# A decoder layer on one core: a front in another order, cross-attention set-up inside the self-attention, the last pair's closing work split

## What is computed

```python
x = x + self_attention(layernorm(x))         # x: 32 sequences x 56 rows x 256; 16 query heads of 128, one key/value head, rotary, causal
x = x + cross_attention(layernorm(x), ctx)   # ctx: 32 x 1500 x 256, with a mask; 16 heads of 16; layernorm of the scaled result
x = x + ffn(layernorm(x))                    # gate, value and output layers of 1024, inputs to 8 bit, weights to -1, 0, 1
```

## Time and profile before

| | |
|---|---|
| median of 3 runs | 1477.72 us (1477.56 to 1482.31) |
| profiled execution, own time | 1479.29 us |
| its span | 1477.5 us |
| granted clock, mean | 0.97 |
| busy: PE, DVE, ACT, POOL | 93%, 68%, 49%, 30% |

### The profile page before, as it was taken

The page is one execution under the profiler, slowest core; times in us unless marked ns, Lnnn a source line. Parts: engine busy times, 40 slices in busy tenths (PEclk is TensorE's granted clock), DMA queues, the critical chain, the costliest instruction groups (busy, mean ns, idle before and its releaser), DMA issues.

```text
span 1477.5 us, 55098 instructions
## 1 busy us (share of the span) xinstructions
PE 1376.1 (93%) x25094; PEld 1176.1 (80%) x25094; DVE 1009.2 (68%) x1786; ACT 717.3 (49%) x939; POOL 442.2 (30%) x394
## 2 busy tenths in 40 slices
PE   3899999999299999999999999999999999999983
PEld 3687777786278888888888888888888888888871
DVE  4666666765044686877778687876877777677765
ACT  1444454443155555464555555555555555555540
POOL 2332232231032323333333333332323233232400
PEclk8899999999689999999999999999999999999995
DMA  7000000000422211212121121211112121111100
GB/s 210 1 2 25 5 1 29 1 2 1 107 58 58 56 50 45 61 31 75 48 59 48 44 62 31 75 50 57 48 44 61 30 76 59 47 48 44 48 6 3
DMA packets 38809, 66.75 MB, mean 45 GB/s; under 512 B 3605, under 2 KB 36818, under 8 KB 38578
## 3 DMA queue, kind: packets, MB, share of 16 engines
q1 hardware_dynamic: 38578, 63.24, 14.7%
HBM read 61.40 MB, written 1.84 MB: 43 GB/s over the span
## 4 chain that ended last, share of the span: by engine, by line
PE 68%; DVE 3%; issue 1%; POOL 0%; POOLq 0%; DVEq 0%
PE proj_ps L1196 19%; PE proj_ps L1187 18%; PE score_ps L1214 13%; PE sum_ps L1234 12%; PE side_ps L1265 3%; PE side_ps L1251 2%; PE side_ps L1279 1%; PE side_ps L1272 1%; PE side_ps L1258 0%; DVE amax L1072 0%; DVE exps L1019 0%; DVE inv L1031 0%; POOL low L894 0%; DVE vals L1010 0%; DVE hidden L1104 0%
## 5 line engine op out<-in xcount | busy, mean ns | idle before, releaser
L954 ACT ACTIVATE exps<-score_ps 125x1792 f32<-125x1792 f32 x192 | 320.6, 1670 | 418.8 <-PE score_ps L1214 418.8
L894 POOL TENSOR_TENSOR low<-raw,high 128x500 fp32r<-128x500 f32 x192 | 293.6, 1537 | 645.1 <-PE proj_ps L1187 510.3
L1019 DVE TENSOR_SCALAR exps<-exps,top 125x896 f32<-125x896 f32 x384 | 288.1, 792 | 18.0 <-ACT exps L954 17.5
L1214 PE MATMUL score_ps<-spread,keys 32*125 32x112 f32 x6144 | 218.9, 279 | 0.9 <-ACT exps L954 0.9
L1234 PEld LDWEIGHTS sum_ps<-exps,vals 125*32 125x32 f32 x12288 | 163.5, 110 | 47.6 <-issue 33.9
L1214 PEld LDWEIGHTS score_ps<-spread,keys 32*125 32x125 f32 x6144 | 184.8, 183 | 16.3 <-ACT exps L954 1.0
L1010 DVE COPY vals<-proj_ps 125x512 f32<-125x512 f32 x192 | 128.3, 688 | 96.8 <-PE proj_ps L1196 96.3
L1234 PE MATMUL sum_ps<-exps,vals 125*32 125x56 f32 x12288 | 192.0, 215 | 0.1
L1196 PE MATMUL proj_ps<-w_h,high 128*125 128x256 f32 x768 | 165.0, 296 | 0.0
L1187 PE MATMUL proj_ps<-high,w_h 128*128 128x500 f32 x384 | 132.8, 427 | 25.4 <-POOL low L894 25.4
L946 ACT ACTIVATE keys<-proj_ps,b_k 128x500 f32<-128x500 f32 x192 | 130.0, 677 | 52.4 <-PE proj_ps L1187 48.0
(11 more groups left out here) (129 smaller groups left out, 1668.2 us busy)
## 6 DMA issues: line engine op xcount, KB each, us to landing
raw<-in_ctxT SPq DMA_DIRECT2D x96, 500.0 KB, 3.7
w_q<-in_attn_Wq SPq DMA_DIRECT2D x4, 512.0 KB, 6.7
w_o<-in_attn_Wo SPq DMA_DIRECT2D x1, 2048.0 KB, 19.9
out<-y_out SPq DMA_DIRECT2D x16, 112.0 KB, 2.0
rows<-in_x SPq DMA_DIRECT2D x1, 1568.0 KB, 14.8
w_raw<-in_ffn_gate_wT SPq DMA_DIRECT2D x1, 1024.0 KB, 8.6
w_raw<-in_ffn_val_wT SPq DMA_DIRECT2D x1, 1024.0 KB, 5.0
w_raw<-in_ffn_out_wT SPq DMA_DIRECT2D x1, 1024.0 KB, 5.8
```

Source lines behind the costliest of these rows:

```text
L894: nc.gpsimd.tensor_tensor(low[r][:, k, :], raw[ring][:, k, :], high[r][:, k, :].bitcast(F32), ALU.subtract).then_inc(low_ready, 1)
L954: nc.scalar.activation(exps[t % 2][:, :, :, :].rearrange("p h r n -> p r h n"), score_ps[0:TILE, :, 0:2 * QW].rearrange("p r (h n) -> p r ...
L1019: nc.vector.tensor_scalar(tile, tile, LIMIT_LO, top[:, n, at:at + 1], ALU.max, ALU.min)\
L1214: ins = nc.tensor.matmul(score_ps[0:TILE, r, to:to + HE * S], keys[c % 2][32 * r:32 * r + 32, k, (at + half) * TILE:(at + half + 1) * TILE ...
```

## The change

In block A, the first load of `x` covers four pairs in place of two, and `w_kv` is loaded ahead of `cos`, `sin` and `causal`. The statistics of group 1 come right behind the keys' rotary, those of group 2 behind query unit 3, and those of group g + 3 in the odd pair of group g (`norm_stats`, with `power1` on POOL). The unit `norm` of group 1 lies between query units 3 and 4. In pair 0, PE works off query units 2 and 3 of group 1 ahead of the first turn. `sines` writes over `swapped` in place of `by_sin`, and `outT` is one buffer in place of two.

Buffers of block B that are filled early now belong to a class `Early`, outside both blocks. The raw buffer of the feed-forward weights is one of them, and holds the first two chunks once the weights are quantised. `w_f` and the small inputs are loaded behind the first raw weights; two memsets move to POOL's start in block A. In pair 15, ACT splits the weights and chunk 0 behind the exponentials (`split_high`), POOL does the low part of chunk 0 and the spreads behind `power(14)`, and DVE does `w_l`, the mask's limits and the scaled bias (`set_up`) behind `norm2_rows(14)`. Block B starts with the load of chunk 2, the high and low part of chunk 1 and PE's first projection.

In block B, `divide(15, 0)` runs at step t = 9 of the last pair, and the four up projections of the last pair go into the four banks of `score_ps` in place of `side_ps`. Three pairs of waits (`wait_apart`) become single waits. The diff, cut to its core:

```diff
+        half = AU // 2
+        units = [("norm", 0), ("kv", 0)] + [("q", 0, u) for u in range(half)] + [("norm", 1)]
+        units += [("q", 0, u) for u in range(half, AU)] + [("kv", 1)]
...
-            sp.dma_start(rows[:, 0:GP, :], x[:, 0:GP, :]).then_inc(x_in[0], 16)
-            for to, of in ((ident, dram["c_ident"]), (gamma, dram["attn_gamma"]), (cos, dram["c_cos"]), (sin, dram["c_sin"]),
-                           (causal, dram["c_causal"])):
+            sp.dma_start(rows[:, 0:2 * GP, :], x[:, 0:2 * GP, :]).then_inc(x_in[0], 16)
+            for to, of in ((ident, dram["c_ident"]), (gamma, dram["attn_gamma"])):
                 sp.dma_start(to[:, :], of).then_inc(small_in, 16)
             sp.dma_start(w_kv[:, :, :], dram["attn_Wkv"].rearrange("(c p) n -> p c n", p=P)).then_inc(wkv_in, 16)
+            for to, of in ((cos, dram["c_cos"]), (sin, dram["c_sin"]), (causal, dram["c_causal"])):
+                sp.dma_start(to[:, :], of).then_inc(small_in, 16)
             for n in range(4):
                 sp.dma_start(w_q[:, :, 512 * n:512 * n + 512], w[:, :, 512 * n:512 * n + 512]).then_inc(wq_in[n], 16)
-            sp.dma_start(rows[:, GP:PAIRS, :], x[:, GP:PAIRS, :]).then_inc(x_in[1], 16)
+            sp.dma_start(rows[:, 2 * GP:PAIRS, :], x[:, 2 * GP:PAIRS, :]).then_inc(x_in[1], 16)
...
+                if n == 0:
+                    for k, name in enumerate(("xattn_WkT", "xattn_WvT")):
+                        sp.dma_start(early.w_f[:, k, :, :], dram[name].rearrange("(c p) n -> p c n", p=P))\
+                          .then_inc(early_w_in, 16)
+                    sp.wait_ge(early_zero, 2)
+                    for to, of in early.loads(dram):
+                        sp.dma_start(to, of).then_inc(early_in, 16)
+            sp.wait_ge(raw_used, 3)
+            for c in range(2):
+                sp.dma_start(early.ring(c), context_chunk(dram, c)).then_inc(early_ctx_in[c], 16)
+            sp.wait_ge(early_ctx_in[1], 16)
...
+            nc.gpsimd.memset(early.b_v[:, :], 0.0).then_inc(early_zero, 1)
+            nc.gpsimd.memset(early.w_xo[:, :, :], 0.0).then_inc(early_zero, 1)
...
+            power1(0)
+            sines(("kv", 0))
+            power1(1)
+            for u in range(AU):
+                sines(("q", 0, u))
+                if u == half - 1:
+                    power1(2)
+            sines(("kv", 1))
...
+                if j and g + 3 < GROUPS:
+                    power1(g + 3)
                 if p:
                     power(p - 1)
+                if p == PAIRS - 1:
+                    early.split_low(nc, pool, early_high)
+                    early.spread_queries(nc, pool, queries)
...
+            norm_stats(GP, 2 * GP)
+            rotary(("q", 0, 0))
+            norm_rows(1)
+            for u in range(1, half):
+                rotary(("q", 0, u))
             dve.wait_ge(x_in[1], 16)
-            norm_stats(GP, PAIRS)
-            norm_rows(1)
-            for u in range(AU):
+            norm_stats(2 * GP, 3 * GP)
+            for u in range(half, AU):
                 rotary(("q", 0, u))
             rotary(("kv", 1))
...
+                if j and g + 3 < GROUPS:
+                    norm_stats(GP * (g + 3), GP * (g + 4))
...
+                    early.set_up(nc, dve, chain, early_w_high, early_in)
...
+                    early.split_high(nc, act, early_w_in, early_w_high, early_ctx_in[0], early_high)
...
+                if u == half:
+                    norm_turn(1)
...
+                if p == 0:
+                    for u in more[2:4]:
...
+    def loads(self, dram):
+        pairs = [(self.mask_i[:, :, :], dram["mask"]),
+                 (self.b_k[:, :], dram["xattn_bk"]),
+                 (self.head_of[:, :], dram["c_head_of"]),
+                 (self.ident_h[:, :], dram["c_ident_h"]),
+                 (self.b_xo[:, :], dram["xattn_bo"].partition_broadcast(ROWS)),
+                 (self.res[:, :], dram["xattn_rs"].partition_broadcast(ROWS)),
+                 (self.ln_gamma[:, :], dram["xattn_gamma"].partition_broadcast(ROWS)),
+                 (self.ln_beta[:, :], dram["xattn_beta"].partition_broadcast(ROWS)),
+                 (self.gate_b[:, :], dram["ffn_gate_b"].partition_broadcast(ROWS)),
+                 (self.val_b[:, :], dram["ffn_val_b"].partition_broadcast(ROWS)),
+                 (self.out_b[:, :], dram["ffn_out_b"].partition_broadcast(ROWS))]
+        for j in range(HJ):
+
+            pairs += [(self.b_v[32 * j:32 * j + HD, :], dram["xattn_bv"][j]),
+                      (self.w_xo[32 * j:32 * j + HD, :, :],
+                       dram["xattn_WoT"].rearrange("(a j d) n -> j d a n", a=HG, j=HJ)[j])]
+        assert len(pairs) == N_EARLY
...
+    def split_high(self, nc, act, w_in, w_high, ctx_in, high_ready):
+
+        act.wait_ge(w_in, 32)
+        for k in range(2):
+            nc.scalar.copy(self.w_h[:, k, :, :], self.w_f[:, k, :, :]).then_inc(w_high, 1)
+        act.wait_ge(ctx_in, 16)
+        for k in range(DC):
+            nc.scalar.copy(self.high[:, k, :], self.ring(0)[:, k, :]).then_inc(high_ready, 1)
+
+    def split_low(self, nc, pool, high_ready):
+
+        for k in range(DC):
+            pool.wait_ge(high_ready, k + 1)
+            nc.gpsimd.tensor_tensor(self.low[:, k, :], self.ring(0)[:, k, :], self.high[:, k, :].bitcast(F32), ALU.subtract)
+
+    def spread_queries(self, nc, pool, queries):
+
+        for n in range(2):
+            for k in range(DC):
+                nc.gpsimd.tensor_tensor(
+                    self.spread[n][:, k, :, :],
+                    queries[:, k, n * S:(n + 1) * S].unsqueeze(1).to_broadcast([P, HE, S]),
+                    self.head_of[:, :].unsqueeze(2).to_broadcast([P, HE, S]), ALU.mult)
+
+    def set_up(self, nc, dve, chain, w_high, loaded):
+
+        dve.wait_ge(w_high, 2)
+        for k in range(2):
+            nc.vector.tensor_tensor(self.w_l[:, k, :, :], self.w_f[:, k, :, :],
+                                    self.w_h[:, k, :, :].bitcast(F32), ALU.subtract)
+        dve.wait_ge(loaded, 16 * N_EARLY)
+        chain(nc.vector.tensor_scalar(self.top[:, :, :], self.mask_i[:, :, :], 0.5, LIMIT_HI, ALU.is_gt, ALU.mult))
+        chain.inc(nc.vector.tensor_scalar(self.top[:, :, :], self.top[:, :, :], LIMIT_LO, None, ALU.add))
+        chain(nc.vector.tensor_scalar(self.res[:, :], self.res[:, :], 0.0, 0.3, ALU.max, ALU.min))
+        chain.inc(nc.vector.tensor_scalar(self.b_xo[:, :], self.b_xo[:, :], self.res[:, 0:1], None, ALU.mult))
...
+            load(2, 0, 2)
...
-                    sp.wait_ge(low_ready, DC * (PC * i + c + 1))
+                    if PC * i + c:
+                        sp.wait_ge(low_ready, DC * (PC * i + c))
...
-            nc.gpsimd.memset(b_v[:, :], 0.0).then_inc(setup_p, 1)
-            nc.gpsimd.memset(w_xo[:, :, :], 0.0).then_inc(setup_p, 1)
             for n in range(2):
                 nc.gpsimd.memset(vals[n][:, :, :, HD:VW], 1.0).then_inc(setup_p, 1)
-            pool.wait_ge(setup_p, 5)
-            pool.wait_ge(small_b, N_SMALL)
+            pool.wait_ge(setup_p, 3)
...
+        def up_ps(p, n):
+
+            return score_ps[0:ROWS, n - 2, :] if p == LAST else side_ps[0:ROWS, :]
...
+                    if last and t == BN + 3:
+                        divide(i, 0)
...
-            for step in tail_steps(LAST, False).values():
-                step()
+            for t, step in tail_steps(LAST, False).items():
+                if t:
+                    step()
...
+                    if p == LAST:
+                        pe.wait_ge(exps_ready, NT * PAIRS)
+                        pe.wait_ge(side_read, SIDES * p + 2)
+                    else:
+                        side(p, n, side_read, SIDES * p + 2)
                     for c in range(DC):
-                        ins = nc.tensor.matmul(side_ps[0:ROWS, :], xqT[:, c, :], w[:, c, 512 * k:512 * k + 512],
+                        ins = nc.tensor.matmul(up_ps(p, n), xqT[:, c, :], w[:, c, 512 * k:512 * k + 512],
...
-            pe.wait_ge(split_w, 4)
-            pe.wait_ge(setup_p, 5)
-            pe.wait_ge(small_b, N_SMALL)
+            pe.wait_ge(setup_p, 3)
```

## The result

The changed kernel took 1445.38 us, the median of four runs (1442.46 to 1447.76), beside 1478.03 for the kernel before on the same chip (1477.56 to 1482.31): a ratio of 0.9772, 95% interval 0.9745 to 0.9798. It is faster, as forecast, by 32.65 us instead of 42, and lies 2.4 us above the range that I gave. The profiled execution took 1444.34 us, with a span of 1442.4.

What follows compares the result with a forecast made beforehand. PE, busy 93% of the span, bounds the kernel, so gains come only where it idles: 13.3 + 3.4 + 22.4 + 0 + 2.2 + 0.8 = 42.1 us. Forecast 1436 us, range 1430.5 to 1443.

Steps and rivals of the forecast that it cites:

- Transition: Change from self-attention to cross-attention: PE's first matmul comes at 387.2 instead of 409.6 us, a gain of 22.4 us.
- rival 3: Second block's start: PE waits for instruction fetch after the branch, 1.1 to 3 us, giving 1437 to 1439 us; chance 0.12.
- Division: Last pair: first divide moved to t = 9 delays last sums about 2.9 us, second divide unmoved; gain 0.
- Up projections: Closing work: four up projections in their own banks take 7.6 instead of 9.8 us, a gain of 2.2 us.
- Front: Start of self-attention: reordered statistics and rotaries bring the first masking to 36 from 49.27 us, a gain of 13.3 us.
- The load delay: Front: larger x load and earlier w_kv delay POOL's first power by 0.8 us, bounds 0 and 2.1.
- 1.65 as the upper of two values: Front: time per rotary if POOL holds it, masking at 37 us; the lower value 1.4 gives 35.5.
- Rival 2: Front held by POOL: slower sines, later loads and a late swap lose 5.6 us, giving 1441.6 us; chance 0.15.
- Pair 0: First pair's turn to pair 1's scores: query units 2 and 3 moved into an earlier wait gain 3.4 us.
- the forecast's own 12.9 us: Pair 0: forecast time from the first masking to the scores of pair 1, previously 16.3 us.
- PE's projection of pair 15 covers all three: Pair 15: early work of ACT (2.2 us), DVE (5.07) and POOL (4.2) is hidden behind PE's projection.
- Heads' projection: Closing work, pair 15: shorter PE pause keeps the clock higher, gain 0.8 us, half of bounds 0 and 1.7.

Runs made afterwards that it cites:

- the best version: Changed kernel plus division at t = 7, first projection before vals wait, later POOL work and sines, front turn-taking, spare matmuls including first block's end: 1430.94 us.

## Why the prediction was wrong

The direction was right, and so was the largest term. What failed is that the moved work was priced by its own length: not by what it does to the operations of the engine beside it, nor by PE's clock. By its own steps, in the profiled executions (forecast 42.1, measured 35.1, so 7.0 missed):

- **Transition, 22.4:** measured 22.47 (24.39 us from the second block's first work to the first projection, now 1.92). The Trainium skill's rule on taken branches (Runtime: NRT & Kernel Launch, section Instruction fetch mechanics) had made rival 3; with the memsets out of the way PE started 0.04 us behind POOL, so no fetch is seen here, and that rival falls as far as these rows show.
- **Division, 0:** the last sums came 3.2 us later and the second divide 2.8 earlier against them. The net cost is 0.4 by these two, and 1.0 beside the run with the division at the end.
- **Up projections, 2.2:** 2.13, by the markers and by putting the bank back.
- **Front, 13.3:** 11.4. The load delay was 0.7 for 0.8. The steps that failed are the durations of DVE's operations, taken at 0.62 and 0.75 where POOL was to work beside them (1.57, 1.57, 1.54). But taking the holds away did not bring the time back: the sines, the sum and the waits between them set the pace, at 1.94 when they take turns. I had 1.65 as the upper of two values and chose 36 between 35.5 and 37; the upper one, and about one more, was true. Rival 2 named this and was half right. The 11.4 has luck in it: over the nine fronts the gain is 8.7 to 11.7, with 10.3 in the middle, by how long the holds are and whether the clock falls.
- **Pair 0, 3.4:** 2.3, and 1.2 of it given back in pairs 1 to 15. Both are the clock, which is down from 47.7 to 54.6 us: the second half's output matmuls take 0.8 longer than the first's (1.86 against 1.07), its turn 0.45 longer (1.11 against 0.66), the scores 1.17. Where the clock stays up the forecast's own 12.9 us (its terms add to 12.8) comes out at 12.7, with spare matmuls and in two profiles without. The forecast priced the clock in the queries, where it held in this profile, and not after them, where a low stretch of the same length stood in the kernel before.
- **"PE's projection of pair 15 covers all three":** this is the step that failed most, by 3.0 us. The cover was there for ACT and for DVE's set-up. But POOL's splits and spreads, priced by their own length only, held the normalising of pair 14 (0.41 to 3.51, after which PE waits 0.9 us for it), and PE's clock fell for a cross query and the last output projection. The rows put 0.4 of it on the hold and 3.1 on the clock, less 0.5 that the last cross query gained. The part of the hold is shown by taking it away. That the early work made the clock fall is not shown: with the hold it stayed up in four profiles of eleven (0.8 to 1.4 us lost, not 3.0), and without the hold, behind the waits of the kernel before, it fell in the one profile that has no spare matmuls there.
- **Heads' projection, 0.8:** -0.1. The pause was halved and the clock fell all the same; I took half of the 1.7 for want of a row, and the low bound was true.
- Beyond the forecast, the steady part of the cross-attention gained 1.5 us: 0.04 in most pairs and 0.9 at once in pair 11. No run was made to find why; the 0.9 is one long pair in the one profile of the kernel before, and stands in none of the sixteen others.

These are 1.9 + 1.1 + 1.2 + 3.0 + 0.9 + 0.4 for the division, less 1.5: 7.0. Another 2.2 us lie between the profiled execution and the median: I went 1.2 under the sum to allow for the median of before, and the median of the changed kernel lies 1.0 above its profiled execution. The clock goes with the time in its four runs: 0.983 in the shortest (1442.46), 0.977 in the longest (1447.76). The version with filled waits spreads over 1.7 us and not 5.3. That fits the same cause, but four or five runs of each are few: the four of the kernel before spread over 4.8.

The ledger of the best version agrees. Against the changed kernel its first projection comes 6.2 us earlier, its first scores 8.3, its last sums 12.1 and its last reduction 13.9. What is added up to the last sums lies in the last pair: from its first sums to its last it is 30.03 us in the changed kernel, 27.13 with the division at t = 7 and 26.27 here.

What stays open: why the clock falls at one of these places in one run and at another in the next, and whether the change made the fall in pair 15 more frequent than it was. Each fall read here stands behind waits of PE, and where the waits were filled (four profiles in pair 15, three in the front and pair 0 with the sines in turn or eight spares) it did not come there. The runs do not show at which wait it decides.

## What to carry to other kernels

Work moved under the cover of a busy engine is free only if it leaves the other engines' operations as long as they were: look in the trace of before for a row where the two engines overlap, and price the moved work by what it does to its neighbour. When PE's waits become short and scattered instead of one long one, price the clock as well: look at the granted clock in the stretches behind every new short wait, in more than one execution, and if it falls, fill the waits with matmuls that nobody reads, a little shorter than the wait. An operation put earlier to get it off the end of a chain wants the step where its own engine has room, not the next one free in the program.

## What the runs showed of the hardware

**POOL holds DVE.** A DVE tensor_scalar of 112x256 took 3.51 us beside POOL's splitting (2.44) and the spreads behind it, in each of eleven profiles, and 0.41 without them in each of five with that work put late; a tensor_tensor of 128x448 took 0.79 to 2.63 beside POOL's sines, mostly 1.5 or 2.6, and 0.62 without. POOL's own sines took 1.1 to 1.3 each there (2.25 for two, 5.18 for four). So it is mostly DVE that pays, and not POOL, as I had feared in rival 2. The Trainium skill (GPSIMD Engine Reference, section Specifications) has the two engines share their SBUF interfaces, with contention for VectorE instructions that read two SBUF inputs or run in a 2-port perf mode. The tensor_tensor reads two, and its rows agree and show how large it can be. The tensor_scalar reads one; no row shows in which mode it ran. The kernel before had such a row already:

```profile
1378.55 2.88 POOL L894 TENSOR_TENSOR low<-raw,high 128x500 fp32r<-128x500 f32 x2 [7.22 <-PE proj_ps L1187]
...
1378.62 3.29 DVE L1019 TENSOR_SCALAR exps<-exps,top 125x896 f32<-125x896 f32 x2
```

The same two operations take 1.27 us when POOL is idle:

```profile
1374.53 1.27 DVE L1019 TENSOR_SCALAR exps<-exps,top 125x896 f32<-125x896 f32 x2
```

**Ten spare matmuls of a few hundred columns are cheap and hold the clock.** They brought 1.8 us at the heads' projection by the markers, and 1.9 at the change of blocks by the totals (1432.88 to 1430.94, the same kernel but for ten spares; the runs of the two do not overlap). Eight of 224 columns take 3.19 us of PE, 0.40 each, so in a wait of 2 us five is the most.
